# A fused FFN, attention and FFN layer: the first layer's fc1 of the next batch placed further ahead in the written order

## The reference

```
x = x + 0.5 * ffn(layernorm(x))          # ffn: layernorm, fc1 128->512, silu, fc2 512->128, + 0.5 z to its residual
x = x + attn(layernorm(x))               # attn below
x = x + 0.5 * ffn(layernorm(x))          # the same weights again
# attn(x): q, k, v = x @ w_qkv in 16 heads of width 8
#   w = relu(q k^T / sqrt(8));  out = (w / (sum(w) + 1e-6)) v
#   y = x + out @ w_out + b_out;  layernorm(y) * gamma + beta
```

## Time and profile before

| | before |
|---|---|
| median of 3 runs | 362.84 us (362.78 to 363.51) |
| the profiled execution's own time | 363.29 us |
| its span, first to last instruction | 361.4 us |
| granted TensorE clock, mean | 1.00 |
| busy: PE, DVE, ACT, POOL | 348.4 us (96%), 269.6 (75%), 224.1 (62%), 210.4 (58%) |
| first scores of batches 0, 1, 2, 3 | 21.88, 60.55, 100.41, 142.25 |
| first scores of batches 4, 5, 6, 7 | 184.10, 225.96, 267.82, 308.83 |

### The profile page before, as it was taken

One profiled execution on the slowest core, in us unless ns is written; L12 is line 12 of the kernel. 1 busy time (PEld: TensorE's weight loads), 2 busy tenths in 40 slices (PEclk: granted clock), 3 DMA queues, 4 the chain that ended last, 5 costly groups with the idle time before them and its releaser, 6 DMA issues.

```text
span 361.4 us, 12662 instructions
## 1 busy us (share of the span) xinstructions
PE 348.4 (96%) x4958; PEld 155.9 (43%) x4958; DVE 269.6 (75%) x670; ACT 224.1 (62%) x408; POOL 210.4 (58%) x445
## 2 busy tenths in 40 slices
...
GB/s 211 11 11 195 56 46 166 93 58 31 163 45 90 33 117 177 31 60 90 133 105 72 21 117 166 40 62 38 128 159 5 2 89 139 98 31 1 3 4 60
DMA packets 22026, 28.48 MB, mean 79 GB/s; under 512 B 3408, under 2 KB 10320, under 8 KB 21968
## 3 DMA queue, kind: packets, MB, share of 16 engines
...
...
## 4 chain that ended last, share of the span: by engine, by line
PE 84%; DVE 8%; ACT 3%; POOL 2%; issue 2%; POOLq 0%; ACTq 0%; DVEq 0%
PE o_bank L769 29%; PE scores L746 14%; PE pre_bank L677 10%; PE pre_bank L684 9%; PE post_bank L677 9%; PE post_bank L684 6%; DVE probs L1321 4%; PE scores L684 3%; PE o_bank L663 2%; ACT post_y L943 1%; DVE k_parts L1156 1%; DVE o_t L1114 1%; ACT probs L1049 1%; POOL norm_x_rs L1354 1%; POOL post_h L1382 0%
## 5 line engine op out<-in xcount | busy, mean ns | idle before, releaser
L1321 DVE TENSOR_SCALAR probs<-scores 128x512 f32<-128x512 f32 x235 | 150.5, 678 | 55.8 <-PE scores L746 52.0
L1049 ACT ACTIVATE probs<-scores 128x512 f32<-128x512 f32 x264 | 142.2, 596 | 64.8 <-PE scores L746 62.8
L769 PE MATMUL o_bank<-probs,v_op 128*32 128x512 f32 x1024 | 135.5, 601 | 0.9 <-ACT probs L1049 0.4
L746 PE MATMUL scores<-q_op,k_op 32*128 32x512 f32 x499 | 69.5, 495 | 0.4 <-DVE q_op L1258 0.4
L746 PEld LDWEIGHTS scores<-q_op,k_op 32*128 32x128 f32 x499 | 27.7, 181 | 84.6 <-issue 52.0
L769 PEld LDWEIGHTS o_bank<-probs,v_op 128*32 128x32 f32 x1024 | 23.4, 108 | 36.0 <-issue 32.5
L943 ACT ACTIVATE pre_y<-pre_bank,b_sum,col_consts 128x512 f32<-128x512 f32 x28 | 21.8, 779 | 21.7 <-PE pre_bank L684 21.7
L1351 POOL TENSOR_SCALAR norm_y_var<-norm_y_mv 128x4 f32<-128x4 f32 x7 | 1.4, 200 | 53.4 <-DVE norm_y_mv L1105 53.4
L677 PEld LDWEIGHTS post_bank<-w,post_y 128*32 128x32 f32 x960 | 26.6, 110 | 11.8 <-issue 11.3
L677 PE MATMUL post_bank<-w,post_y 128*32 128x128 f32 x960 | 31.1, 273 | 0.0
L677 PEld LDWEIGHTS pre_bank<-w,pre_y 128*32 128x32 f32 x960 | 26.4, 110 | 10.3 <-issue 7.8
...
## 6 DMA issues: line engine op xcount, KB each, us to landing
...
out_dram<-o_rows ACTq DMA_DIRECT2D x7, 256.0 KB, 2.4
pre_x<-in_x_dram ACTq DMA_DIRECT2D x6, 256.0 KB, 2.7
pre_past<-pre_blocks SPq DMA_DIRECT2D x6, 256.0 KB, 2.4
pre_t<-pre_past SPq DMA_DIRECT2D x24, 64.0 KB, 2.0
post_past<-post_blocks SPq DMA_DIRECT2D x5, 256.0 KB, 2.0
post_t<-post_past SPq DMA_DIRECT2D x20, 64.0 KB, 2.4
```

Source lines behind the costliest of these rows:

```text
L746: mm(score_bank(b, s, i, j), k_op[rows, g, P * kt:P * (kt + 1)], q_op[rows, g, :], start=True, stop=True).then_inc(scores_done[i], 1)
L769: last = mm(o_bank[pair][VW * j:VW * (j + 1), :], v_op[:, kt, heads_of(g).start + 2 * j, :], probs[:, s % 2, j, :], start=(odd == 0 and kt ...
L1049: activation(probs[:, s % 2, 2 * i + j, :], score_bank(b, s, i, j), ACT.Relu).then_inc(probs_done[i][j], 1)
L1321: v.tensor_scalar(probs[:, s % 2, 2 * i + j, :], score_bank(b, s, i, j), 0.0, None, ALU.max).then_inc(probs_done[i][j], 1)
```

## The change

The order is changed, and the engine of eight relus (below); else each instruction of before stands somewhere in after. The order in which fills take the banks, of which the semaphore counts are made, was a rule by batch, and is a list now (`PRE_SEQUENCE`, `POST_SEQUENCE`).

- **Batch 0.** Steps 7, 8 and 9 had no fill. They get fc1.0, fc1.1, fc1.2 of batch 2, steps 14 and 15 its fc1.3 and fc2.0. For that the load of x for batch 2 stands at the end of ACT's first part, its statistics in DVE's step 1, the turn in step 3.
- **Batch 1.** The turn for batch 3 moves from DVE's step 3 to step 1; step 3 is without a fill; steps 4 to 6 hold fc1.0 to fc1.2 of batch 3, and step 15 fc1.3. Before, steps 6, 7 and 8 had no fill, and four steps had two; now two steps have two.
- **Batches 2 to 6.** They start at fc2.0 of the next batch, where before they started at fc1.1. fc1.0 and fc1.1 of the batch behind it stand early in steps 8 and 9; uT stays early in step 10; k and q move from early to late. The steps with two fills are 2 and 12 to 15 (before 2, 5, 12, 14, 15). In batch 6, which has no fc1 of a later batch to do, steps 8 and 9 have no fill.
- **Three banks for ACT** in steps 3 and 6 of batches 2 to 6 (none before), 3, 5, 6 of batch 1 (before 6, 7, 8), 7 and 8 of batch 0 (before 7, 8, 12, 13). x1 and its statistics move from DVE's steps 6 and 7 to 4 and 6.

The diff, cut to its core (the tables of ACT and DVE follow those of PE):

```diff
--- before.py
+++ after.py
@@ -37,7 +37,14 @@
+PRE_SEQUENCE = (
+    [(fill, 0) for fill in FIRST_FILLS] + [(fill, 1) for fill in PRE_FILLS[:6]]
+    + [entry for b in range(1, B) for entry in (
+        [(f"fc1.{f}", b + 1) for f in range(3 if b < 3 else 2) if b + 1 < B]
+        + [(fill, b) for fill in ("uT", "k", "q", "v")]
+        + [(fill, b + 1) for fill in (PRE_FILLS[4:6] if b < 3 else PRE_FILLS[3:6]) if b + 1 < B])])
 PRE_BY_DMA, POST_BY_DMA = range(2, B), range(1, B - 2)
+POST_SEQUENCE = [(fill, b) for b in range(B) for fill in POST_FILLS if not (fill == "hT" and b in POST_BY_DMA)]
...
-THREE_BY_ACT = {0: (7, 8, 12, 13), 1: (6, 7, 8), B - 1: (0, 1, 2, 3, 4, 8, 9, 10, 14)}
+THREE_BY_ACT = {0: (7, 8), 1: (3, 5, 6), **{b: (3, 6) for b in range(2, B - 1)}, B - 1: (0, 1, 2, 3, 4, 8, 9, 10, 14)}
...
 PE_ORDER = [
-    ([], ["pre.fc1.1@1"]),
-    ([], ["pre.fc1.2@1"]),
...
-    (["pre.k@1"], []),
-    (["pre.q@1"], ["post.fc1.0@-1"]),
...
+    (["pre.fc1.0@2"], []),
+    (["pre.fc1.1@2"], []),
     (["pre.uT@1"], []),
+    ([], ["pre.k@1"]),
+    ([], ["post.fc1.0@-1", "pre.q@1"]),
...
 ACT_FIRST = [
...
-    "first.uT.0", "first.uT.1", "first.k0.0", "first.q0.0", "first.q0.1", "first.v.0", "first.k0.1"
+    "first.uT.0", "first.uT.1", "first.k0.0", "first.q0.0", "first.q0.1", "first.v.0", "first.k0.1", "pre.load_x@2"
...
+    ["pre.fc1.0@2", "post.y_apply@-1"],
...
 DVE_START = [
     ["first.k_lo.1"],
-    ["first.q_lo.1"],
-    [],
-    [],
-    ["pre.x_stats@2"],
-    [],
-    ["pre.turn@2", "pre.x1@1"],
+    ["first.q_lo.1", "pre.x_stats@2"],
+    [],
+    ["pre.turn@2"],
+    [],
+    [],
+    ["pre.x1@1"],
...
 DVE_SECOND = [
     ["oT.1@-1", "den.1@-1"],
-    ["a.1@-1", "aT@-1"],
+    ["a.1@-1", "aT@-1", "pre.turn@2"],
...
 POOL_SECOND = [
-    "v_in.2", "post.u_bias", "pre.x_stats@2", "pre.x_apply@2", "post.y_stats@-1", "post.y_gamma@-1", "pre.x1_stats@1",
-    "pre.u_apply@1", "v_in.3", "post.x2_stats@-1", "post.x_apply@-1", "pre.x1_beta@1", "post.xr@-1", "pre.xr@2",
-    "v_in.0@1", "v_in.1@1"
+    "v_in.2", "post.u_bias", "post.y_stats@-1", "post.y_gamma@-1", "pre.x1_stats@1", "pre.u_apply@1", "v_in.3",
+    "post.x2_stats@-1", "post.x_apply@-1", "pre.x1_beta@1", "post.xr@-1", "pre.xr@2", "v_in.0@1", "v_in.1@1"
 ]
...
             def base(self, b):
 
-                return sum(len(self.fills_of(i)) for i in range(b))
+                return sum(batch < b for _, batch in self.sequence)
 
             def after(self, fill, b):
 
-                return self.base(b) + self.fills_of(b).index(fill) + 1
+                return self.sequence.index((fill, b)) + 1
```

More of the change, by code:

```diff
@@ L60 @@
     (["pre.fc2.1@1", "pre.fc2.2@1"], ["pre.fc2.3@1"]),
[L61 to L67, removed]
     ([], ["pre.fc1.0@2"]),
     ([], ["pre.fc1.1@2"]),
+    ([], ["pre.fc1.2@2"]),
+    ([], ["pre.uT@1"]),
+    (["pre.k@1"], []),
+    (["pre.q@1"], []),
+    ([], ["pre.v@1"]),
+    ([], ["pre.fc1.3@2"]),
+    ([], ["pre.fc2.0@2"]),
 ]
 PE_SECOND = [
-    ([], ["pre.fc1.2@1"]),
-    ([], ["pre.fc1.3@1"]),
-    ([], ["post.op@-1", "pre.fc2.0@1"]),
     ([], ["pre.fc2.1@1"]),
     ([], ["pre.fc2.2@1"]),
-    (["pre.fc2.3@1"], []),
+    ([], ["post.op@-1", "pre.fc2.3@1"]),
     ([], []),
[L79 to L82, removed]
-    (["pre.q@1"], ["post.fc1.0@-1"]),
+    ([], ["pre.fc1.0@2"]),
+    ([], ["pre.fc1.1@2"]),
+    ([], ["pre.fc1.2@2"]),
+    ([], ["pre.uT@1"]),
+    (["pre.k@1"], []),
+    (["pre.q@1"], []),
+    ([], ["post.hT@-1", "pre.v@1"]),
+    ([], ["post.fc1.0@-1"]),
     ([], ["post.fc1.1@-1"]),
-    ([], ["pre.v@1"]),
     ([], ["post.fc1.2@-1"]),
-    (["post.fc1.3@-1"], ["pre.fc1.0@2"]),
+    ([], ["post.fc1.3@-1"]),
+    ([], ["pre.fc1.3@2"]),
 ]
 PE_ORDER = [
-    ([], ["pre.fc1.1@1"]),
-    ([], ["pre.fc1.2@1"]),
-    ([], ["post.op@-1", "pre.fc1.3@1"]),
     ([], ["pre.fc2.0@1"]),
     ([], ["pre.fc2.1@1"]),
-    (["pre.fc2.2@1", "pre.fc2.3@1"], []),
+    ([], ["post.op@-1", "pre.fc2.2@1"]),
+    ([], ["pre.fc2.3@1"]),
     ([], ["post.fc2.0@-2"]),
@@ L98 @@
     ([], ["post.fc2.2@-2"]),
-    (["post.fc2.3@-2"], []),
+    ([], ["post.fc2.3@-2"]),
+    (["pre.fc1.0@2"], []),
+    (["pre.fc1.1@2"], []),
     (["pre.uT@1"], []),
-    (["pre.k@1"], []),
[L102 to L105, removed]
+    ([], ["pre.k@1"]),
+    ([], ["post.fc1.0@-1", "pre.q@1"]),
+    ([], ["post.fc1.1@-1", "pre.v@1"]),
+    ([], ["post.fc1.2@-1", "pre.fc1.2@2"]),
+    ([], ["post.fc1.3@-1", "pre.fc1.3@2"]),
 ]
 POST_BANK_STEPS = (5, 7, 9, 11, 13)
-THREE_BY_ACT = {0: (7, 8, 12, 13), 1: (6, 7, 8), B - 1: (0, 1, 2, 3, 4, 8, 9, 10, 14)}
+THREE_BY_ACT = {0: (7, 8), 1: (3, 5, 6), **{b: (3, 6) for b in range(2, B - 1)}, B - 1: (0, 1, 2, 3, 4, 8, 9, 10, 14)}
 PE_END = [
@@ L142 @@
     ["pre.hT@1", "first.q.1", "pre.fc1.0@1"],
-    ["pre.fc1.1@1", "pre.load_x@2"],
+    ["pre.fc1.1@1"],
     ["pre.fc1.2@1"],
@@ L146 @@
     [],
-    [],
-    [],
-    [],
     ["pre.load_x@3"],
+    ["pre.fc1.0@2"],
+    ["pre.fc1.1@2"],
+    ["pre.fc1.2@2"],
     ["pre.uT@1"],
@@ L154 @@
     ["pre.v@1"],
-    ["pre.fc1.0@2"],
-    ["pre.fc1.1@2"],
+    ["pre.fc1.3@2"],
+    [],
 ]
 ACT_SECOND = [
-    ["pre.fc1.2@1"],
-    ["pre.fc1.3@1", "pre.load_x@3"],
-    [],
+    [],
+    [],
+    ["pre.load_x@3"],
+    [],
+    ["pre.fc1.0@2", "post.y_apply@-1"],
+    ["pre.fc1.1@2"],
+    ["pre.fc1.2@2"],
+    ["pre.uT@1"],
+    ["pre.k@1"],
+    ["pre.q@1"],
+    ["post.hT@-1", "pre.v@1"],
+    ["post.fc1.0@-1"],
+    ["post.fc1.1@-1"],
+    ["post.fc1.2@-1"],
+    ["post.fc1.3@-1"],
+    ["pre.fc1.3@2"],
+]
+ACT_ORDER = [
+    [],
+    [],
+    ["pre.load_x@3"],
     [],
@@ L166 @@
     [],
[L167 to L186, removed]
+    ["pre.fc1.0@2"],
+    ["pre.fc1.1@2"],
     ["post.store@-2", "pre.uT@1"],
     ["pre.k@1"],
[L189 to L192, removed]
+    ["post.fc1.0@-1", "pre.q@1"],
+    ["post.fc1.1@-1", "pre.v@1"],
+    ["post.fc1.2@-1", "pre.fc1.2@2"],
+    ["post.fc1.3@-1", "pre.fc1.3@2"],
 ]
@@ L231 @@
     [],
-    ["oT.0", "den.0"],
-    ["a.0", "pre.k_lo@1"],
+    [],
+    ["pre.k_lo@1"],
     ["pre.q_lo@1"],
     ["pre.x_stats@3"],
-    [],
-    [],
+    ["oT.0", "den.0"],
+    ["a.0"],
 ]
```

25 lines of the change are left out of this document (10 added, 15 removed).

## The result

The changed kernel takes **367.15 us** (median of 4 runs, 366.72 to 369.20) against 362.81 (362.54 to 363.51): a ratio of 1.0128, with a 95% interval of 1.0087 to 1.0168. It is slower, by 1.3%; 361.9 was predicted.

A forecast was written before the change was run, and what follows sets the result against it. PE, 96% busy, was taken as the bound, with only waiting beyond 1.42 a step and 0.87 a fill to win. Terms -2.0 - 1.36 + 1.25 + 1.2 = -0.9 from 362.84 gave 361.9 us, range 359.9 to 363.9.

The forecast's parts named there:

- Batches 2 to 5 (-0.49 each): uT starts 0.55 sooner, now waiting for POOL's u; behind it +0.06; four batches give -2.0 us.
- batch 6 (-1.36): uT starts 0.55 sooner on the same POOL chain, with 0.81 less waiting behind it: -1.36 us.
- Batch 1 (+1.2): PE stalls 1.3 at fc1.0 for turned rows; uT -0.3, uT to batch end +1.55: +1.2 us.
- From there to the rows' landing: ... 6.3: Batch 1, turn's end to rows landed: issue 0.34, first hop's wait 2.2, reads' issue 1.73, last landing 2.0.
- fc1.0 from 72.9 to 73.8: Batch 1, step 4: fc1.0 starts when the rows land, then silu to 74.7, y_apply 1.65, uT at 81.6.
- if the rows land by 71.6: Lower bound of batch 1's term: 0 if the rows land by then, when step 4's values end.
- rival 3: Batch 1: load of x and turn collide, first hop up to 2.7 later; sum +1.8, 364.6 us; chance 0.13.
- Batch 0 (+1.25): Waits of 1.96 gone; three fills (2.60), k and q early (0.3, 0.2), DVE's step 3 (0.1) added; +0.9 to +1.9.
- rival 4: Three relus and a silu overfill steps 7, 8 of batch 0 and 5, 6 of batch 1: +1.2, 363.1 us; chance 0.10.
- 361.0 to 362.9, the bounds of batches 0 and 1 on either side: Span given to the forecast itself, apart from its rivals; chance 0.45.

The follow-up runs named there:

- e_turn_early: Changed kernel with batch 1's turn one step earlier on DVE, at the end of step 0's row: 363.84 us, ratio 1.0032 to the kernel before.
- e_turn_y: Changed kernel with batch 1's turn in step 0 and y_apply ahead of fc1.0's silu in step 4: 362.36 us, ratio 0.9989 to the kernel before.
- v5: Changed kernel with batch 1's turn in step 0, y_apply before silu, batch 3's load in batch 0's step 9, uT behind values in batches 2 to 6: 359.68 us.
- e_load3_late: Changed kernel with the load of batch 3's rows in step 9 of batch 0 instead of step 6: 366.74 us, ratio 1.0114 to the kernel before.

## Why the prediction was wrong

- **Batches 2 to 5 (-0.49 each) and batch 6 (-1.36): right**, with -0.42 to -0.45 and -1.30. The mechanism too: uT waits for POOL's u, and the waits of steps 12 and 15 are gone.
- **Batch 1 (+1.2): the step that failed**, +4.69. "From there to the rows' landing: ... 6.3": the turn ended at 68.43 and the reads landed at 76.25, 7.8 later. The 2.2 that I took for the first hop's wait is a mean over hops of two kinds, some alone and some beside a fetch, and this one was of the long kind (3.9). I had the 3.0 in the earlier trace rows and did not ask which hops were long. So the stall was 2.58, not 1.3.
- **Same term: "fc1.0 from 72.9 to 73.8".** It took 1.93 at the lower clock. I had counted a stall of TensorE as lost time alone. Against the forecast (moved by the 1.77 that batch 1 starts later) fc1.0 began 1.7 late, its length added 1.0 and the chain through ACT and POOL to u 0.5: uT 3.25 late, nearly the whole error.
- **The bound of 0 "if the rows land by 71.6"** failed as well. In e_turn_early fc1.0 waits for nothing, and batch 1 is still 1.50 over before: PE comes to fc1.0 0.7 later in the batch than forecast, and from there to uT it takes 9.33 (74.03 to 83.36) and not the 8.7 of the forecast. So the loss was not the landing's alone: y_apply behind the silu has a price without any stall, and in e_turn_y, where it stands ahead, batch 1 is 2.0 shorter.
- **What the parts are worth** in batch 1, by one profile each: rows late, clock fallen, y_apply behind: 44.54; clock kept: 43.55; y_apply first as well: 41.69; rows early too: 39.33. So 1.0 for the clock, 1.9 for the order on ACT, 2.4 for the landing. The shares hang on the order in which they are taken: the early turn alone, which ends the wait and with it the fall of the clock, is worth 3.2 (44.54 to 41.35), and the order then 2.0 (41.35 to 39.33). With the clock fallen the order showed nothing (44.63), in a profile whose clock stayed low twice as long.
- **The prediction's rival 3** (load and turn collide) had the sign and some of the size (+1.8), but not the cause: the load gone, the hop still took 4.13. Its point of decision, a landing 8.0 after the turn, was not reached (7.8); the lower clock and the order on ACT made the rest of the loss. The Trainium skill (Trainium Kernel Development and Optimization, section Key Constraints) has DMAs issued by SP, ACT and POOL run on the same 16 engines and interleave. The traces agree in v5 (3.34 beside the load and q's copies); in batch 1 of the changed kernel this was not what counted.
- **Batch 0 (+1.25): too small**, +2.32. 0.6 is step 7, whose rows came late (0.39 of wait), which I had put four steps off and safe. Without that (e_load3_late) it is +1.73, inside my bounds: step 3 lost 0.29 and not 0.1, steps 7 to 9 took 0.13 over three fills.
- **The prediction's rival 4** (three relus and a silu) is not what costs steps 5 and 6: in e_turn_y, with the same relus, they take 2.29 and 2.55. The 0.26 that step 6 keeps over 2.29 is about the 0.29 that the rival asked for a step.
- **The range.** "361.0 to 362.9, the bounds of batches 0 and 1 on either side" does not follow from those bounds: +0.9 to +1.9 and 0 to +2.0 give 360.4 to 363.4 with the other terms as they stand. The 367.15 lies outside both.

**Where the expected gain went.** It came, 3.05 us in batches 2 to 6, and was paid twice over at the start: three fills done ahead in batch 0, of which batch 6 gives back half, and a stall in batch 1 that also took the clock.
